# A routed expert layer inside a six-part decoder: logits moved into the normalisation, token numbers made by TensorE, rows fetched by number

## The reference

```python
h = _layernorm(x, ln_w, ln_b)
logits = h @ router_w
expert_idx = jnp.argmax(logits, axis=-1)
...
for e in range(E):
    gv = h @ expert_wv[e]
    gate_raw, value = jnp.split(gv, 2, axis=-1)
    y = gate_raw * jax.nn.sigmoid(gate_raw) * value @ expert_proj[e]
    out = out + jnp.where((expert_idx == e)[..., None], y, 0.0)
```

## Time and profile before

| | before |
|---|---|
| median of 3 runs | 2673.68 us (2667.2 to 2674.04) |
| the profiled execution | 2665.48 us, of which the span of instructions is 2663.7 us |
| mean granted TensorE clock | 0.965 |
| busy share of the span | TensorE 85%, VectorE 74%, ScalarE 68%, GpSimd 49% |
| the experts, from their normalisation to the last result's copy | about 2124 to 2413 us |

### The profile page before, as it was taken

The page is one execution under the profiler, slowest core; times in us unless marked ns, Lnnn a source line. Parts: engine busy times, 40 slices in busy tenths (PEclk is TensorE's granted clock), DMA queues, the critical chain, the costliest instruction groups (busy, mean ns, idle before and its releaser), DMA issues. The chain is left out here.

```text
span 2663.7 us, 38653 instructions
## 1 busy us (share of the span) xinstructions
PE 2261.7 (85%) x12380; PEld 1168.0 (44%) x12381; DVE 1966.2 (74%) x1854; ACT 1824.1 (68%) x2848; POOL 1316.4 (49%) x517
## 2 busy tenths in 40 slices
PE   7788888888888888888888896879968979998988
PEld 2344444444434444444444342422422356665547
DVE  6899999999978999999999367772493222225655
ACT  5999999999959999999999344117405631112256
POOL 2199998999933999989999111000000040110010
PEclk8999999999999999999999978979989989999999
DMA  2510001000015000010000021001001160011000
GB/s 99 139 38 28 24 28 44 27 25 28 24 74 135 27 28 28 28 40 28 28 28 16 19 76 55 1 1 49 17 1 34 33 250 22 22 68 38 0 11 32
DMA packets 58297, 112.66 MB, mean 42 GB/s; under 512 B 13251, under 2 KB 19267, under 8 KB 57168
## 3 DMA queue, kind: packets, MB, share of 16 engines
q1 hardware_dynamic: 49408, 98.24, 12.0%
q0 software_dynamic: 8784, 13.03, 1.6%
HBM read 84.97 MB, written 25.97 MB: 42 GB/s over the span
## 5 line engine op out<-in xcount | busy, mean ns | idle before, releaser
L1493 POOL TENSOR_TENSOR hs<-hs,c_bc 128x2048 f32<-128x2048 f32 x256 | 1166.4, 4556 | 61.2 <-DVE hs L1544 45.7
L1544 DVE TENSOR_TENSOR_SCAN hs<-decays,ps 128x512 f32<-128x512 f32 x512 | 610.7, 1215 | 27.4 <-ACT decays L1507 8.8
L1544 DVE TENSOR_TENSOR_SCAN hs<-decays,carry,ps 128x512 f32<-128x512 f32 x512 | 621.6, 1269 | 5.6 <-PE ps L1571 4.6
L1579 PE MATMUL ps<-hs,sel 128*64 128x512 f32 x2048 | 496.4, 605 | 16.5 <-POOL hs L1493 16.2
L1571 PE MATMUL ps<-ident,dbu_even 128*128 128x128 f32 x2048 | 296.6, 284 | 96.3 <-DVE hs L1544 64.0
L1571 PE MATMUL ps<-ident,dbu_odd 128*128 128x128 f32 x2048 | 294.8, 283 | 92.2 <-DVE hs L1544 61.5
L1507 ACT ACTIVATE decays<-delta_far,A 128x512 f32<-128x512 f32 x512 | 355.5, 706 | 7.3 <-DVE hs L1544 7.1
L1507 ACT ACTIVATE decays<-delta_near,A 128x512 f32<-128x512 f32 x512 | 355.8, 706 | 1.5 <-DVE hs L1544 1.5
L1515 ACT ACTIVATE dbu_odd<-du_turned,b_turned 128x512 f32<-128x512 f32 x512 | 355.5, 706 | 0.0
L1515 ACT ACTIVATE dbu_even<-du_turned,b_turned 128x512 f32<-128x512 f32 x496 | 344.4, 706 | 0.0
L1571 PEld LDWEIGHTS ps<-ident,dbu_even 128*128 128x128 f32 x2048 | 221.0, 142 | 246.3 <-DVE hs L1544 193.9
(11 more groups left out here) (325 smaller groups left out, 2616.2 us busy)
## 6 DMA issues: line engine op xcount, KB each, us to landing
c_bc<-c_rows SPq DMA_DIRECT2D x256, 128.0 KB, 2.8
o_rows<-osb SPq DMA_DIRECT2D x26, 256.0 KB
u_rows<-u SPq DMA_DIRECT2D x4, 1024.0 KB, 4.5
d_rows<-delta SPq DMA_DIRECT2D x4, 1024.0 KB, 4.2
delta_near<-d_rows SPq DMA_DIRECT2D x4, 1024.0 KB, 10.0
hs<-u_rows SPq DMA_DIRECT2D x4, 1024.0 KB, 6.7
delta_far<-d_rows SPq DMA_DIRECT2D x4, 1024.0 KB, 13.3
w_down<-in_expert_proj SPq DMA_DIRECT2D x1, 4096.0 KB, 38.9
```

Of the source, the lines that this page charges most:

```text
L1493: pool.tensor_tensor(x, x, spread(c_bc[:, g, :], 4), ALU.mult).then_inc(weighed.sem, 1)
L1544: dve.tensor_tensor_scan(hs[:, quad % RING, n, :], decays[:, s % RING, :], ps[:, DBU + s % RING, :], carry[:, at(i * GB, g), blk] if q els ...
L1579: mm = pe.matmul(ps[lo:lo + DB, ACC + quad % 2 * 2 + j // 2, :], k.sel2[:, :], hs[:, quad % RING, j, :], start=False, stop=False, skip_gro ...
```

## The change

1. In every normalisation with a mean and no arriving input, and in `norm_twice`, GpSimd adds the two channel groups of chunks 1 to 3 (into the space for the squares), and TensorE sums the mean of those chunks with one product in place of two.
2. The experts' `norm` issues the router's weights first, and TensorE makes the logits inside its block, chunk by chunk (`Router`), in place of the 10 filler products. Weight and bias of chunks 0, 2 and 3 go to VectorE, chunk 1 stays with ScalarE.
3. `sort_tokens` counts after four of the eight groups of turns. SyncE stores the rows in token order to `xs` as they come, and three more small steps of VectorE split the slot into tile and row. GpSimd has nothing to do there: the sum of `X` and `H2` moves into `run_tiles`.
4. Before, 19 blank tiles were written to `xs`; now one tile of 128 rows, which blank slots point to.
5. In `run_tiles` the 16 scatters, the row products of `first_x` and the integer copies of token numbers go. VectorE builds a table of which token number stands in which tile, TensorE multiplies it with `lands` (16 products with 19 columns), and three small steps make the number of every slot. GpSimd fetches the rows of each tile from `xs` by these numbers, all 19 of them, and scatters the results by them. TensorE loads the experts' numbers (L2521 before) ahead of that.
6. The linear attention's weights are issued after the third tile. The loads of `ys` are issued by SyncE at the end of the `run_tiles` block, and into `H2`; the filler products are 5 and stand at that block's end too.

```diff
         def _(pe):
             def means(c):
+                if c and joins:
+                    pe.wait_ge(halves_joined.sem, halves_joined.at(c))
+                    pe.matmul(ps[:, c, :], k.inv[:, :], sq[:, c, 0, :], start=True, stop=True).then_inc(mean_ready.sem, 1)
+                    return
...
                 pe.wait_ge(centred.sem, centred.at(NCH))
-                keep_busy(k, pe, 0, 10)
+                for c in range(NCH):
+                    if c == 1:
+                        pe.wait_ge(normed.sem, normed.at(C))
+                    else:
+                        pe.wait_ge(normed_dve.sem, normed_dve.at(C * max(1, c)))
+                    router.logits(pe, c)
...
+            def affine_chunk(c):
+                if c < BY_POOL:
+                    dve.wait_ge(scaled.sem, scaled.at(c + 1))
+                else:
+                    dve.wait_ge(scaled_dve.sem, scaled_dve.at(c - BY_POOL + 1))
+                for b in range(C):
+                    x = dst[:, b, c * W:(c + 1) * W]
+                    dve.tensor_scalar(x, x, weight[:, b:b + 1], bias[:, b:b + 1], ALU.mult, ALU.add)\
+                       .then_inc(normed_dve.sem, 1)
+
             def finish(c):
+                if affine and c == BY_POOL:
+                    affine_chunk(0)
                 invert(c)
                 if c >= BY_POOL:
                     scale(c)
+                    if affine:
+                        affine_chunk(c)
...
             if affine:
-                for c in range(NCH):
-                    affine_chunk(c)
+                affine_chunk(1)
...
         @block.gpsimd
         def _(pool):
-            if arrives:
-                arrives.fetch(pool)
+            for c in range(1, joins + 1):
+                pool.tensor_tensor(sq[:, c, 0, :], src[:, 0, c * W:(c + 1) * W], src[:, 1, c * W:(c + 1) * W],
+                                   ALU.add).then_inc(halves_joined.sem, 1)
...
+              .then_inc(self.here[c].sem, 16)
 
     def turn(self, pe, c):
-        if c == 0:
-            keep_busy(self.k, pe, 2 * NCH - 1, 7)
...
-        norm(k, H2, HN, weight=vec[:, :, 2], bias=vec[:, :, 3],
-             loads=[(wr[:], a["router"]), (before[:], a["before"]), (counts[:], a["tile_counts"]),
+        router = Router(k, HN, wr, a["router"])
+        norm(k, H2, HN, weight=vec[:, :, 2], bias=vec[:, :, 3], router=router,
+             loads=[(before[:], a["before"]), (counts[:], a["tile_counts"]),
                     (ids[:], a["token_ids"]),
-                    (xs, k.empty[:].rearrange("p (a d) -> p a d", a=1).broadcast_to([P, NT, D + 1]))],
+                    (k.xs[N:N + P, :], k.empty[:, 0:D])],
...
+
+    def fetch(self, sp):
+        sp.dma_start(self.wr[:], self.source).then_inc(self.weights.sem, 16)
+
+    def logits(self, pe, chunk):
+        pe.wait_ge(self.weights.sem, self.weights.at(16))
+        for t in range(chunk * W // P, (chunk + 1) * W // P):
+            for c in range(C):
+                mm = pe.matmul(self.k.ps[:, 0, t * E_:(t + 1) * E_], self.HN[:, c, t * P:(t + 1) * P], self.wr[:, c, :],
...
 
+                def count():
+                    pe.wait_ge(picked.sem, picked.at(1))
+                    flat = pick[:].rearrange("p t e -> p (t e)")
+                    pe.matmul(ps[:, 1, 0:TT * E_], before[:], flat, start=True, stop=True)
+                    pe.matmul(ps[:, 1, TT * E_:2 * TT * E_], ones[:], flat, start=True, stop=True)\
+                      .then_inc(counted.sem, 1)
+
                 for g in range(TT // 2):
+                    if g == 4:
+                        count()
                     turn(g)
-                pe.wait_ge(picked.sem, picked.at(1))
-                flat = pick[:].rearrange("p t e -> p (t e)")
-                pe.matmul(ps[:, 1, 0:TT * E_], before[:], flat, start=True, stop=True)
-                pe.matmul(ps[:, 1, TT * E_:2 * TT * E_], ones[:], flat, start=True, stop=True).then_inc(counted.sem, 1)
 
...
+            @block.sync
+            def _(sp):
+                for g in range(TT // 2):
+                    sp.wait_ge(rows_in.sem, rows_in.at(g + 1))
+                    sp.dma_start(k.xs[2 * g * P:(2 * g + 2) * P, :].rearrange("(t p) d -> p t d", p=P),
+                                 rows[:, 2 * g:2 * g + 2, 0:D]).then_inc(rows_stored.sem, 16)
...
                 step(dve.tensor_tensor(place[:], place[:], pick[:].rearrange("p t e -> p e t"), ALU.mult))
                 step(dve.tensor_reduce(slot_f[:], place[:].rearrange("p e t -> p t e"), AX.X, ALU.add))
-                step(dve.tensor_copy(slot[:], slot_f[:]))
-        for s in (logits_ready, picked, counted, added, id_in_row):
+                step(dve.tensor_copy(k.slot[:], slot_f[:]))
+                step(dve.tensor_scalar(k.slot[:], k.slot[:], P - 1, None, ALU.bitwise_and))
+                step(dve.tensor_copy(row_of[:], k.slot[:]))
...
-            for t in range(N // P):
-                pool.indirect_dma_start(k.xs, bass.IndirectOffsetOnAxis(ap=slot[:, t:t + 1], axis=0),
-                                        rows[:, t, :], None).then_inc(scattered.sem, 16)
-
...
+            def fetch(c):
+                p = c % 2
+                if c >= 2:
+                    pool.wait_ge(x_turned.sem, x_turned.at(c - 1))
+                pool.indirect_dma_start(xrow[:, p, :], None, k.xs,
+                                        bass.IndirectOffsetOnAxis(ap=token[:, c:c + 1], axis=0)).then_inc(x_here[p].sem, 16)
+
+            def store(c):
+                p = c % 2
+                pool.wait_ge(y_copied.sem, y_copied.at(c + 1))
+                if c:
+                    pool.wait_ge(y_stored[1 - p].sem, y_stored[1 - p].at(16 * ((c + 1) // 2)))
+                pool.indirect_dma_start(k.ys, bass.IndirectOffsetOnAxis(ap=token[:, c:c + 1], axis=0),
                                         yrow[:, p, :], None).then_inc(y_stored[p].sem, 16)
...
+            pool.wait_ge(rows_stored.sem, rows_stored.at(16 * TT // 2))
+            pool.wait_ge(tokens_known.sem, tokens_known.at(3))
+            fetch(0)
+            fetch(1)
+            pool.tensor_tensor(X[:], X[:], H2[:], ALU.add).then_inc(added.sem, 1)
+            fetch(2)
             for c in range(NT):
-                if c + 1 < NT:
-                    take_id(Beat(None, c + 1), (c + 1) % 2)
-                store(Beat(None, c), c % 2)
+                if c + 3 < NT:
+                    fetch(c + 3)
+                store(c)
+            pool.wait_ge(added.sem, added.at(1))
...
+            sp.wait_ge(rows_stored.sem, rows_stored.at(16 * TT // 2))
+            sp.wait_ge(x_turned.sem, x_turned.at(3))
+            for dst, source in late:
+                sp.dma_start(dst, source).then_inc(late_in.sem, 16)
+            sp.wait_ge(late_in.sem, late_in.at(16 * len(late)))
             for p in range(2):
                 sp.wait_ge(y_stored[p].sem, y_stored[p].at(16 * ((NT + 1 - p) // 2)))
-            sp.wait_ge(late_in.sem, late_in.at(16 * len(late)))
+            sp.wait_ge(added.sem, added.at(1))
+            gathered.fetch(sp)
...
-            def first_x():
-
-                for c in range(C):
-                    for t in range(N // P):
-                        if c == 0:
-                            pe.wait_ge(landed.sem, landed.at(t + 1))
-                        mm = pe.matmul(ps[:, XT, c * P:(c + 1) * P], rows[:, t, c * P:(c + 1) * P], lands[:, t, :],
-                                       start=(t == 0), stop=(t == N // P - 1))
-                mm.then_inc(x_turned.sem, 1)
+            def tokens():
+
+                for t in range(TT):
+                    pe.wait_ge(landed.sem, landed.at(t + 3))
+                    mm = pe.matmul(ps[:, OUT, 0:NT], lands[:, t, :], id_in[:, t, :], start=(t == 0), stop=(t == TT - 1))
+                mm.then_inc(ids_summed.sem, 1)
...
-            first_x()
-            pe.wait_ge(weights_in.sem, weights_in.at(32))
             first = Beat(None, 0)
             e = experts_of(first, FIRST + 1)
+            tokens()
+            turn_x(first, 0)
+            pe.wait_ge(weights_in.sem, weights_in.at(32))
             gate_value(first, 0, 0, e[0])
...
+            keep_busy(k, pe, XT, 5)
 
         @block.scalar
         def _(act):
...
+            def each(ap, pattern, **kw):
+                return ap.rearrange(pattern, **kw).broadcast_to([P, TT, NT])
+
+            dve.tensor_tensor(id_in[:], each(tile_of[:], "p (t a) -> p t a", a=1),
+                              each(numbers[:, P:P + NT], "p (a s) -> p a s", a=1), ALU.is_equal).then_inc(landed.sem, 1)
+            dve.wait_ge(landed.sem, landed.at(1))
+            dve.tensor_tensor(id_in[:], id_in[:], each(ids[:, 0:TT], "p (t a) -> p t a", a=1), ALU.mult)\
+               .then_inc(landed.sem, 1)
+            for t in range(TT):
+                dve.tensor_scalar(lands[:, t, :], numbers[:, 0:P], row_of[:, t:t + 1], None, ALU.is_equal)\
+                   .then_inc(landed.sem, 1)
...
```

(2 more changed lines are left out.)

178 lines of the change are left out of this document (86 added, 92 removed).

## The result

The changed kernel takes **2654.09 us**, the median of 6 runs (2652.77 to 2660.08), against 2669.50 us of 6 runs of the kernel before beside it (2664.79 to 2674.04). The ratio is 0.9939, with a 95% interval from 0.9923 to 0.9955: 16.3 us less, between 12.0 and 20.6. The forecast was 2649.7 us and a gain of 24. The time lies in the range of the forecast, but part of that is the base: the forecast started from a median of three runs, 2673.7, and six give 4.2 us less. The gain itself was 8 us too large, and the time alone could not tell the forecast from its rivals: 2654.1 lies between the forecast's 2649.7 and the rivals' 2657 (half the slip of the rows) and 2659.7 (the gap stays). The traces tell them apart. The profiled execution of the changed kernel took 2654.03 us, its span is 2652.2.

The account below looks back on a forecast made before the run. The prediction took TensorE to bound the tiles and a chain of waits the stage before them. Start 17, end 4 and other normalisations 3 sum to 24 us: 2673.7 - 24 = 2649.7 us, range 2640 to 2664.

Parts of the forecast that it names:

- half the slip of the rows: Before the first expert product: row stores at 94 GB/s land late, 2665.3 us, half that slip 2657; rows late had chance 0.11.
- the gap stays: Before the first expert product: the unexplained 10.1 us remain, so the gain is 14 us and the time 2659.7; chance 0.13.
- three rivals: Around experts' start and tiles: unexplained 10.1 us stay (0.13), rows land late (0.11), fetches hold the tiles, slower (0.03).
- The sign that I had set for being wrong: A wait of 5 us or more in front of the first expert product, or TensorE idle in the tiles.
- The three other normalisations: `norm_twice`, second cross attention and feed-forward: joined sums save 1 us each, 3 us in all, bounds 0 and 8.
- The end: End of the experts: SyncE loads results at once, linear attention's first turns come sooner; 4 us off, bounds 2 and 6.
- the 17 us of the start: Experts' normalisation to first expert product: first product at 2172.4 against 2189.56, 17 us off.
- The logits end at 2149.8: Experts' normalisation: three quarters of logits before VectorE's end at 2146.8, last quarter 3.0 us at slow clock; 9.9 us sooner.
- Then 16 products, 32 records, the first half at 0.19 and the rest at 0.109: 4.8: Token numbers at the tiles' block start: TensorE's products take 4.8 us, half of them at slow clock; numbers at 2167.7.
- Rows landed: 2168.6. This sets the time; that wait is new.: Before the first fetch: rows land in `xs` behind the weights, 0.9 us after the token numbers, and set the time.
- Numbers to first product: Token numbers at 2167.7 to first product at 2172.4: 0.9 rows wait, fetch 2.4 and 0.3, turn 0.4, copy 0.4, hand-overs 0.3.
- the forecast's own case, 2658: Whole kernel, main case with chance 0.70: with the bounds alone the time reaches from 2640 to 2658 us.

Follow-up runs that it names:

- the second execution of before: The kernel before, unchanged, profiled once more: 2672.14 us in one run.
- the second executions: The kernel before and the changed kernel, both unchanged, each profiled once more: 2672.14 us and 2640.06 us, one run each.
- the second experiment: Kernel before with only SyncE loading `ys` inside the experts' last block and five fillers there: 2659.99 us against 2669.1, ratio 0.9970.
- experiment 6: Changed kernel, register loads behind the token numbers, fillers sized at 0.86 us each: 2642.74 us; with overstaying fillers taken out, 2643.44 us, ratio 0.9887.

## Why the prediction was right or wrong

**Right: the sign and the place of each part.** The logits ran in the normalisation, the counts between the turns, the tiles kept their time (223.2 us from first product to last copy before, 223.7 after; 228.6 in the second execution of before, with its wait for the second tile), none of the three rivals came about: no gap stands in either trace of the changed kernel, the rows were not late, no fetch held a tile. The sign that I had set for being wrong, a wait of 5 us in front of the first product, is met only across the barrier: of TensorE's 7.04 us of idle time ahead of the token numbers 3.7 lie at the end of the sort and 3.4 in the register loads. Inside the block the longest wait is that of 4.45 us for the fetch. The three other normalisations gave 0.4, 1.4 and 1.3 us where I had 1 each. The end gave 5.3 us from the last copy of a result to the first mean (15.9 to 10.6; 16.7 and 9.6 in the second executions) where I had 4; the second experiment shows the same 5 by itself.

**Wrong: the 17 us of the start.** From the normalisation's start to the first expert product it is 65.3 us before, 48.1 in my working and 54.1 in the trace: 11 us less where I had 17. The 6 us between the last two, by my steps:

- *"The logits end at 2149.8"*, 25.5 us from the start: 28.3 in the trace. VectorE's end came 0.5 us late. The other 2.3 are the step "the last quarter, 16 records, 3.0": not one quarter runs at 1.2 GHz but three, and they stand behind each other, so the last ends 5.3 us behind VectorE.
- *"The next block at 2159.0"*, 9.2 us after the logits: 9.6.
- *"Then 16 products, 32 records, the first half at 0.19 and the rest at 0.109: 4.8"*: all 32 at 1.2 GHz, 7.01 us (3.93 at full clock, experiment 6). With it the numbers stood 11.1 us after the block's start, in place of 8.7. These two steps are the ones that failed: I had put the low clock on one quarter of the logits and on half of the token numbers, and it lay on three quarters and on all of them. Together they are 4.5 of the 6 us.
- *"Rows landed: 2168.6. This sets the time; that wait is new."* The landing was right: 38.9 less 7.4 gave 31.5 us for the last weights, 31.8 were measured, and the rows came 5.5 us behind them (6.5). But the numbers came 8 us later than the rows in the trace (2179.2 against 2171.0), so no wait for rows stood there. The rule that I had drawn on, of the Trainium skill's page "DMA: Bandwidth & Descriptors", section "Queues, rings and completion order", says that each ring consumes its descriptors in order, and not that they finish in order. The trace agrees with it: the first row store was issued at 2160.59 and landed at 2166.1, 0.6 us behind the last weights.
- *Numbers to first product*, 4.7 us with 0.9 of waiting for rows in it: 5.1, of which 0.85 between VectorE's CAST and GpSimd's issue and 2.8 of the fetch, where I had 0.3 and 2.4.

**Wrong in its ground: the gap.** The sum took the 10.1 us between the last product on rows and ScalarE's copy as time that the kernel spends, and asked only whether it would come back. The runs show that it was an event of one execution. Without it the wait for the second tile's rows appears, so an ordinary execution of before is 6 us shorter at the second tile than the profiled one. It is this that the sum should have been made against: there the changed kernel gains 7 to 9 us in normalisation and sort (45.5 or 47.2 to 37.9 or 38.4), loses up to 1 in the tiles' block (244.4 against 245.4 and 244.6), gains 6 to 7 in the linear attention's normalisation and 3 in the others, and loses 1.4 in the linear attention's own block (32.1 to 33.4): there, in code that is the same, the granted clock was 0.79 between 2492 and 2500 us against 1.00 before. The block took 33.4 or 33.5 us in three of nine profiled executions with the changed end and 32.1 in the other six, so I do not put it down to the change. With the ranges that makes 14 to 18 us; the whole stage, from the experts' normalisation to the end, gives 17.1 to 17.6 in every pairing of the two executions of each kernel, and 16.3 were measured.

The two mistakes did not cancel, they add: 6 us too much at the start, 4.5 of them for the clock, and about 2 more for the gap (normalisation, sort and tiles together take 293.7 us in the first execution of before and 291.6 in the second), against 1 to 3 too little at the end. That the time still fell into the range owes something to its width: its upper end for the forecast's own case, 2658, follows from no sum shown, since 17 + 2 + 0 gives 2654.7.

## What to carry to other kernels

A stall that no record explains should be looked for in a second execution before a sum rests on it; here it hid, in addition, the wait that would have stood in its place. When work is taken out of TensorE's queue and small products are left standing in waits, price them at the lower of its two clock levels, all of them and the first large ones behind them. Fillers that ended with the wait they filled gave the clock back around the token numbers (7.0 us to 3.9, and a first tile at full clock), though not in the last quarter of the logits; one that outlasts its wait costs its full length, so take its length from a row of the same kernel first. A change in several parts needs the parts run alone, or at least read block by block: here normalisation and sort (7 to 9 us, 1.8 of them by the joined sums) and the end (5) carried the gain, and the part with the most new code, numbers by TensorE and fetched rows, gained nothing in its block until its loads and its clock were mended. Only the end and the joined sums were run without the rest; what the logits and the counts give alone is read from the blocks and was not tested.

## What the runs showed of the hardware

- One stall of 10.1 us between TensorE's last product and the copy of its result, in 1 of 6 profiled executions of the kernel before and its variants, without a record that explains it. Its cause stays open.
- The granted clock fell from 1.00 to 0.50 in products with 4 columns although the records show TensorE busy without a pause (10.32 of 10.40 us). With large fillers among them it fell too, behind the first 32 records (0.59 in the window of the fillers that follow), and came back in the fillers; it was 1.00 in the two quarters behind.
- A pair of VectorE's multiply-adds beside GpSimd's multiplication took 3.03 or 3.04 us in place of 1.00 in all eight profiled executions of the changed kernel and its variants.
- Two executions of the changed kernel differed by 14 us (2654.03 and 2640.06), almost all of it ahead of the experts, in steps of 1.5 to 4 us in single blocks. From the experts on they differed by 0.3 us. A part worth less than that can be read from its own block, and not from one run's time.
